# Layers 1 and 2 of a graph network: loops replaced by written-out instructions on four engines

## The chip, the cores and the metric

One core of one Trainium2 chip. The time is the device time of one launch in microseconds (us), the median of several runs. In rows and text PE is TensorE's matmul and PEld its weight load, DVE is VectorE, ACT is ScalarE, POOL is GpSimd and SP is SyncE; a q behind the name is the engine's sequencer.

## The reference

```python
def sage(h, w_self, w_neigh, b):
    agg = segment_sum(h[src], dst, num_segments=n) * inv_deg
    return h @ w_self + agg @ w_neigh + b
h = relu(layernorm(x))                 # 100000 nodes x 128
h = relu(sage(h, ws0, wn0, b0))        # 128 -> 256
h = relu(sage(h, ws1, wn1, b1))        # 256 -> 256
out = x + sage(h, ws2, wn2, b2)        # 256 -> 128
```

The graph has 150000 edges sorted by target: 50000 between random nodes and one from each node to itself. All numbers are float32.

## The kernel before

The kernel is written per engine: each engine has one instruction stream, and semaphores order them. The nodes are cut into 392 pairs of 2 x 128 nodes. Layer 0 goes through the pairs and writes, per node, the two products p (for neighbours) and q (for the node itself) to a table in HBM. Layer 1 does the same with that table and writes z and y. Layer 2 goes through 264 triples of 3 x 128 nodes and writes the output. A preamble (until about 80 us) finds each tile's edges between different nodes; these are few, so that one gather of 128 rows serves a tile in layers 0 and 1, and two gathers serve a triple in layer 2.

In layer 1 a pair passes through these steps, by line:

- VectorE copies the pair's two columns of row numbers into one of four `gather_at` slots (L1146). It first waits until the gathers of the slot's last use have landed.
- GpSimd starts two indirect gathers with them (L646), into one of four `nbr` slots, after TensorE has summed that slot's last rows. SyncE loads the pair's own q rows (L484).
- ScalarE builds a selection matrix (L802, L810) and splits the gathered rows in a high part (L723); VectorE makes the low part (L1156).
- TensorE multiplies with the selection (L1539, L1540, L1543: 4 matmuls), VectorE scales and adds the own rows (L1166), TensorE transposes (L1566: 4), ScalarE and VectorE split the result (L826, L1325), and TensorE does the dense product with W2 (L1445: 12 matmuls of high and low parts).
- ScalarE and VectorE take z and y out of PSUM (L817, L1336) and SyncE stores them (L509).

The engines run these steps of different pairs at once: in one turn TensorE handles pairs n, n-3 and n-1, VectorE n, n-4, n-5, n-7 and n-9. In layer 2 VectorE copies row numbers at L1353, GpSimd gathers at L659, TensorE sums (L1580, L1583), VectorE adds (L1361, L1366, L1378), and ScalarE's queue stores.

All streams are in program order. How a stream is laid out is decided by two helpers: `peeled` writes a step out once for each pair, with constant addresses and constant semaphore counts; `looped` puts four steps (one per slot) in a hardware loop, where the pair number is a register, so that addresses and counts are worked out by register instructions. `pipeline` writes out the first `rounds` times four steps, loops over the rest, and writes out the tail of `lag` steps.

In the kernel before SyncE's stream is written out in all layers. The other four engines use `pipeline` in layers 1 and 2, with `rounds` 2 (GpSimd, TensorE, ScalarE in layer 2), 3 (ScalarE in layer 1, VectorE in layer 2) or 4 (VectorE in layer 1). Layer 0 has loops of its own. Between the layers every store of one layer is waited for before the next begins its gathers, and a branch on a flag skips code for graphs of a more general kind.

Of the kernel before, what the change touches and what calls it, by code (L numbers as in the profile page):

```python
# [20 lines left out]
PAIRS = -(-N_NODES // (PAIR * SLOTS)) * SLOTS  # L21
# [4 lines left out]
TRIPLES = -(-NODE_TILES // (3 * SLOTS)) * SLOTS  # L26
# [50 lines left out]
def peeled(step, first, last, total, slots=SLOTS):  # L77

    for n in range(first, last):
        step(Step(n // slots, n % slots, total, False, slots))  # L80


def looped(eng, step, first_use, last_use, total, slots=SLOTS):

    with eng.Fori(first_use, last_use) as i:
        for slot in range(slots):
            step(Step(i, slot, total, True, slots))


def pipeline(eng, step, total, lag, rounds=2, slots=SLOTS):  # L90

    assert lag < rounds * slots and total % slots == 0
    peeled(step, 0, rounds * slots, total, slots)
    looped(eng, step, rounds, total // slots, total, slots)
    peeled(step, total, total + lag, total, slots)


def build(nc, x, src, dst, dst_starts, windows, ws0, wn0, b0, ws1, wn1, b1, ws2, wn2, b2, out):
# [14 lines left out]
    with ExitStack() as ctx:  # L113
# [274 lines left out]
        def triple_rows(table, s):  # L388

            return table.rearrange("(j r) f -> r j f", j=3)[bass.ds(s.n * P, P), :, :]  # L390
# [136 lines left out]
        def _(pool):  # L527
# [63 lines left out]
            def general(pass_no):  # L591
                with pool.If(pool.value_load(general_flag[0:1, 0:1], min_val=0, max_val=1) != 0):
                    general_sums(pass_no)
# [44 lines left out]
            def gathers(layer, table, rows_in, freed, width):  # L638
                def gather(s):
                    if s.has(SLOTS):  # L640

                        pool.wait_ge(freed, s.back(SLOTS).n + 1)
                    pool.wait_ge(layer.index_copied, s.n + 1)
                    pool.sem_inc(pool_may_go, 1)
                    for j in range(2):
                        pool.indirect_dma_start(rows_in[s.slot][0:SLOT_ROWS, j, 0:width], None, table,  # L646
                                                bass.IndirectOffsetOnAxis(gather_at[s.slot][0:SLOT_ROWS, j:j + 1], axis=0),
                                                bounds_check=last_half_row, oob_is_err=False
                                                ).then_inc(layer.gathered[s.slot], 16)
                pipeline(pool, gather, PAIRS, 0)  # L650

            def triple_gathers(s):
                if s.has(SLOTS):
# [21 lines left out]
            all_stored(pool, L0.stored, SLOT_USES)  # L675
            general(1)
            gathers(L1, p_table, nbr, L1.summed, H)
            all_stored(pool, L1.stored, SLOT_USES)
            general(2)
            pipeline(pool, triple_gathers, TRIPLES, 0)  # L680

        @block.scalar
        def _(act):
# [112 lines left out]
            def layer1(first):  # L796
# [24 lines left out]
                if t.live():  # L821

                    act.wait_ge(L1.turned, t.n + 1)
                    if t.has(2):
                        act.wait_ge(L1.dense_done, t.back(2).n + 1)
                    act.activation(hid_hi[t.half][:, :, :], l1_turn[t.half].rearrange("p (k n) -> p k n", k=2),  # L826
                                   ACT.Relu).then_inc(L1.hi_ready, 1)
            pipeline(act, layer1, PAIRS, 5, rounds=3)


            def layer2(s):
# [14 lines left out]
                if u.live():  # L846
                    act.wait_ge(L2.rows_ready, u.n + 1)
                    act.dma_start(triple_rows(out, u), triple_out[u.slot]).then_inc(L2.stored[u.slot], 16)
            pipeline(act, layer2, TRIPLES, 3)

        @block.vector
        def _(dve):
# [307 lines left out]
            def means(layer, s, width, added):  # L1160

                dve.wait_ge(layer.summed, s.n + 1)
                if s.has(2):
                    dve.wait_ge(layer.turned, s.back(2).n + 1)
                for j in range(2):
                    last = dve.scalar_tensor_tensor(agg[s.half][:, j, 0:width],  # L1166
                                                    row_sums[s.slot][:, j * H:j * H + width],
                                                    inv_degree[:, bass.ds(s.n * 2 + j, 1)],
                                                    added[:, j, 0:width], op0=ALU.mult, op1=ALU.add)
                last.then_inc(layer.agg_ready, 1)  # L1170
# [144 lines left out]
            def layer1(first):  # L1315
# [25 lines left out]
                if s.live():  # L1341
                    dve.wait_ge(L1.own_loaded[s.slot], (s.use + 1) * 16)
                    means(L1, s, H, own[s.slot])
            pipeline(dve, layer1, PAIRS, 9, rounds=4)

            general(2)

# [31 lines left out]
                                      ALU.add).then_inc(L2.rows_ready, 1)  # L1379
            dve.tensor_copy(b2_held, b2_rows[:, :]).then_inc(L2.b2_put, 1)  # L1380
            dve.wait_ge(L2.b2_put, 1)
            pipeline(dve, layer2, TRIPLES, 6, rounds=3)

        @block.tensor
        def _(pe):
# [141 lines left out]
            def layer1(s):  # L1527
# [31 lines left out]
                if t.live():  # L1559
# [6 lines left out]
                            last = nc.tensor.matmul(l1_turn[t.half][:, at:at + P], agg[t.half][:, j, m * P:(m + 1) * P],  # L1566
                                                    ident[:, :], is_transpose=True, start=True, stop=True)
                    last.then_inc(L1.turned, 1)
            pipeline(pe, layer1, PAIRS, 3)

            general(2)

            def layer2(s):
# [10 lines left out]
                                            triple_select[s.half][:, SHARED + j, :],  # L1584
                                            triple_rows_in[s.slot][:, j, :], start=j == 0, stop=j == SHARED - 1)
                last.then_inc(L2.summed, 1)
            pipeline(pe, layer2, TRIPLES, 0)


INPUTS = ["x", "src", "dst", "dst_starts", "windows", "L0_gnn_ws0", "L0_gnn_wn0", "L0_gnn_b0", "L0_gnn_ws1", "L0_gnn_wn1", "L0_gnn_b1",  # L1590
# [36 lines left out]
```

## Time and profile before

| what | value |
|---|---|
| median of 3 runs | 3845.57 us (3840.11 to 3855.55) |
| profiled execution, its own time | 3837.3 us |
| its span in the trace | 3835.5 us |
| instructions recorded | 100978 |
| busy share PE / PEld / DVE / ACT / POOL | 91 / 82 / 87 / 80 / 67% |
| HBM read and written | 451 and 361 MB |
| granted clock of TensorE, mean | 0.923 |

Times in the trace count from the start of the span. An engine is busy while it executes; register, branch and semaphore instructions and the issue of plain transfers are not counted as busy. The granted clock is a share of TensorE's 2.4 GHz. "issue" as what ended an idle time means that the engine waited for nothing that the profile shows.

### The profile page before, as it was taken

Reading aid. Unit: us, or ns where it says so; the run is one execution under the profiler, and the core shown is the slowest. Engines: PE = TensorE matmul, PEld = TensorE weight load, DVE = VectorE, ACT = ScalarE, POOL = GpSimd, SP = SyncE. Lnnn points to the kernel's source line nnn. Section 1 sums busy time; section 2 is a strip of 40 time slices with the busy share of each in tenths; the row PEclk is TensorE's granted clock in tenths of the full one; section 3 lists DMA queues with packets and bytes.
Section 4 is the critical chain, followed back from the end, with each engine's and each line's share of the span. In section 5 each row is a group of like instructions: output and inputs, shape, how many; then the busy total and the mean of one; then the engine's idle time right before and its main releaser. Section 6 shows DMA issues by size and latency. Waiting matters only on the chain. (4 is left out here: it accounts for less than half of the span.)

```text
span 3835.5 us, 100978 instructions
## 1 busy us (share of the span) xinstructions
PE 3503.3 (91%) x22513; PEld 3162.4 (82%) x22513; DVE 3342.0 (87%) x9695; ACT 3085.1 (80%) x8036; POOL 2557.9 (67%) x3691
## 2 busy tenths in 40 slices
PE   1999999999999999999998999999999986777777
PEld 1888888888888888888887999998999976666666
DVE  7999999999999999999986888988988977777777
ACT  4888888888888888888886877878887867777777
POOL 2666666666666666666555777777777767777776
PEclk9999999999999999999999999999999986566555
DMA  2444444444444444444444888888888879999998
GB/s 75 138 143 143 144 142 144 143 144 144 144 143 144 143 142 143 142 143 144 141 145 143 247 245 247 249 248 244 247 246 246 249 216 263 262 262 266 262 265 249
DMA packets 828104, 727.99 MB, mean 190 GB/s; under 512 B 90198, under 2 KB 699614, under 8 KB 827918
## 3 DMA queue, kind: packets, MB, share of 16 engines
q1 hardware_dynamic: 642069, 570.14, 45.9%
q0 software_dynamic: 80336, 104.91, 11.5%
q10 hardware_dynamic: 105600, 51.92, 4.5%
q8 instruction: 26, 0.43, 0.1%
q14 instruction: 73, 0.59, 0.0%
HBM read 451.32 MB, written 361.23 MB: 212 GB/s over the span
## 5 line engine op out<-in xcount | busy, mean ns | idle before, releaser
L1445 PE MATMUL ps_out<-w_hi,hid_hi 128*128 128x512 f32 (+1 forms) x3136 | 1142.3, 364 | 27.3 <-DVE layer_mem L1336 24.7
L610 POOL DMA_INDIRECT loaded_rows<-in_x,gather_at x784 | 904.0, 1153 | 390.2 <-issue 241.7
L1445 PE MATMUL ps_out<-w_hi,hid_lo 128*128 128x512 f32 (+1 forms) x3136 | 1054.6, 336 | 0.0
L1445 PE MATMUL ps_out<-w_lo,hid_hi 128*128 128x512 f32 (+1 forms) x3136 | 1049.7, 335 | 0.0
L646 POOL DMA_INDIRECT layer_mem<-pq_rows,gather_at x784 | 788.2, 1005 | 273.2 <-issue 215.7
L1445 PEld LDWEIGHTS ps_out<-w_hi,hid_hi 128*128 128x128 f32 x3136 | 589.3, 188 | 135.4 <-issue 51.6
L659 POOL DMA_INDIRECT layer_mem<-zy_rows,gather_at x528 | 526.0, 996 | 182.3 <-issue 141.3
L1445 PEld LDWEIGHTS ps_out<-w_hi,hid_lo 128*128 128x128 f32 x3136 | 588.8, 188 | 68.8
L1445 PEld LDWEIGHTS ps_out<-w_lo,hid_hi 128*128 128x128 f32 x3136 | 591.1, 188 | 55.1
L750 ACT ACTIVATE layer_mem<-ps_hid,b_col 128x256 f32<-128x256 f32 x784 | 329.1, 470 | 211.4 <-PE ps_hid L1445 193.7
L837 ACT ACTIVATE layer_mem<-iota_row,triple_node 128x128 f32<-128x128 f32 x1056 | 337.3, 390 | 154.3 <-DVE layer_mem L1378 57.5
L1445 PE MATMUL ps_hid<-cat_hi,w_hi 128*128 128x256 f32 x1568 | 438.5, 280 | 3.6 <-DVE cat_lo L1251 3.4
L1445 PE MATMUL ps_hid<-cat_lo,w_hi 128*128 128x256 f32 x1568 | 435.6, 278 | 0.0
L1445 PE MATMUL ps_hid<-cat_hi,w_lo 128*128 128x256 f32 x1568 | 435.2, 278 | 0.0
L1325 DVE SCALAR_TENSOR_TENSOR hid_lo<-ps_out,hid_hi 128x512 fp32r<-128x512 f32 x392 | 270.6, 690 | 102.9 <-ACT hid_hi L826 90.6
L779 ACT ACTIVATE h_own<-loaded_rows,shift,rstd 128x128 f32<-128x128 f32 x784 | 340.8, 483 | 3.4 <-POOL shift L623 3.3
L1184 DVE BATCH_NORM_STATS2 stats<-loaded_rows 128x6 f32<-128x256 f32 x784 | 300.4, 424 | 48.3 <-DMA loaded_rows<-in_x,gather_at 28.4
L779 ACT ACTIVATE h_nbr<-loaded_rows,shift,rstd 128x128 f32<-128x128 f32 x784 | 340.8, 483 | 0.0
L723 ACT ACTIVATE nbr_hi<-layer_mem 128x256 fp32r<-128x256 f32 x392 | 163.1, 416 | 220.9 <-DMA layer_mem<-pq_rows,gather_at 219.1
L1240 DVE SCALAR_TENSOR_TENSOR layer_mem<-layer_mem,self_scale,ps_out 128x256 f32<-128x256 f32 x784 | 334.4, 467 | 0.9 <-issue 0.7
L1445 PEld LDWEIGHTS ps_hid<-cat_hi,w_hi 128*128 128x128 f32 x1568 | 295.1, 188 | 26.7 <-DVE cat_lo L1251 11.4
L1445 PEld LDWEIGHTS ps_hid<-cat_lo,w_hi 128*128 128x128 f32 x1568 | 295.0, 188 | 17.0
(172 smaller groups left out, 8817.2 us busy)
## 6 DMA issues: line engine op xcount, KB each, us to landing
pq_rows<-layer_mem SPq DMA_DIRECT2D x392, 512.0 KB, 3.2
loaded_rows<-pq_rows SPq DMA_DIRECT2D x392, 256.0 KB
zy_rows<-layer_mem SPq DMA_DIRECT2D x392, 256.0 KB
loaded_rows<-zy_rows SPq DMA_DIRECT2D x264, 192.0 KB, 4.1
layer_mem<-in_x SPq DMA_DIRECT2D x264, 192.0 KB
out_rows<-layer_mem ACTq DMA_DIRECT2D x264, 192.0 KB
loaded_rows<-in_x SPq DMA_DIRECT2D x392, 128.0 KB, 2.2
loaded_rows<-in_x,gather_at POOLq DMA_INDIRECT x784, 2.9
```

Of the source, the lines that this page charges most:

```text
L610: pool.indirect_dma_start(raw[s.slot][0:rows, 2 + j, :], None, table, bass.IndirectOffsetOnAxis(gather_at[s.slot][0:rows, j:j + 1], axis=0 ...
L646: pool.indirect_dma_start(rows_in[s.slot][0:SLOT_ROWS, j, 0:width], None, table, bass.IndirectOffsetOnAxis(gather_at[s.slot][0:SLOT_ROWS, ...
L659: pool.indirect_dma_start(triple_rows_in[s.slot][:, j, :], None, z_table, bass.IndirectOffsetOnAxis(gather_at[s.slot][:, j:j + 1], axis=0) ...
L723: act.activation(nbr_hi[s.half][:, 0:tiles, 0:width], nbr[s.slot][:, 0:tiles, 0:width], ACT.Copy).then_inc(layer.nbr_hi_ready, 1)
L750: last = act.activation(h1[t.half][:, m, :], ps_hid[t.half][:, m * PAIR:(m + 1) * PAIR], ACT.Relu, bias=b0_col[:, m:m + 1])
L779: last = act.activation(rows, raw[t.slot][:, j, :], ACT.Relu, bias=shift[t.half][:, j:j + 1], scale=rstd[t.half][:, j:j + 1])
L837: last = act.activation(triple_distance[s.half][:, b, :], iota_row[:, :], ACT.Abs, scale=-1.0, bias=triple_node[:, bass.ds(s.n * (2 * SHAR ...
L1184: last = dve.bn_stats(stats[t.half][:, k, :], raw[t.slot][:, 2 * k:2 * k + 2, :].rearrange("p j f -> p f j"))
L1240: last = dve.scalar_tensor_tensor(q_out[t.slot][:, j, :], p_out[t.slot][:, j, :], self_scale[:, bass.ds(t.n * 2 + j, 1)], ps_out[t.half][: ...
L1325: dve.scalar_tensor_tensor(hid_lo[t.half][:, :, :], l1_turn[t.half].rearrange("p (k n) -> p k n", k=2), 0.0, hid_hi[t.half][:, :, :].bitca ...
L1445: ins = nc.tensor.matmul(o, a, b, start=n == 0, stop=n == len(terms) - 1)
```

## The change

Eight calls of `pipeline` become calls of `peeled` over all pairs or triples and the tail: GpSimd's, ScalarE's, VectorE's and TensorE's streams of layers 1 and 2 are written out from first to last. Steps, their order on each engine, the semaphores and the buffers stay the same. Layer 0 and SyncE's stream are not touched.

```diff
--- before.py
+++ after.py
@@ -647,7 +647,7 @@
                                                 bass.IndirectOffsetOnAxis(gather_at[s.slot][0:SLOT_ROWS, j:j + 1], axis=0),
                                                 bounds_check=last_half_row, oob_is_err=False
                                                 ).then_inc(layer.gathered[s.slot], 16)
-                pipeline(pool, gather, PAIRS, 0)
+                peeled(gather, 0, PAIRS, PAIRS)
 
             def triple_gathers(s):
                 if s.has(SLOTS):
@@ -677,7 +677,7 @@
             gathers(L1, p_table, nbr, L1.summed, H)
             all_stored(pool, L1.stored, SLOT_USES)
             general(2)
-            pipeline(pool, triple_gathers, TRIPLES, 0)
+            peeled(triple_gathers, 0, TRIPLES, TRIPLES)
 
         @block.scalar
         def _(act):
@@ -825,7 +825,7 @@
                         act.wait_ge(L1.dense_done, t.back(2).n + 1)
                     act.activation(hid_hi[t.half][:, :, :], l1_turn[t.half].rearrange("p (k n) -> p k n", k=2),
                                    ACT.Relu).then_inc(L1.hi_ready, 1)
-            pipeline(act, layer1, PAIRS, 5, rounds=3)
+            peeled(layer1, 0, PAIRS + 5, PAIRS)
 
 
             def layer2(s):
@@ -846,7 +846,7 @@
                 if u.live():
                     act.wait_ge(L2.rows_ready, u.n + 1)
                     act.dma_start(triple_rows(out, u), triple_out[u.slot]).then_inc(L2.stored[u.slot], 16)
-            pipeline(act, layer2, TRIPLES, 3)
+            peeled(layer2, 0, TRIPLES + 3, TRIPLES)
 
         @block.vector
         def _(dve):
@@ -1341,7 +1341,7 @@
                 if s.live():
                     dve.wait_ge(L1.own_loaded[s.slot], (s.use + 1) * 16)
                     means(L1, s, H, own[s.slot])
-            pipeline(dve, layer1, PAIRS, 9, rounds=4)
+            peeled(layer1, 0, PAIRS + 9, PAIRS)
 
             general(2)
 
@@ -1379,7 +1379,7 @@
                                       ALU.add).then_inc(L2.rows_ready, 1)
             dve.tensor_copy(b2_held, b2_rows[:, :]).then_inc(L2.b2_put, 1)
             dve.wait_ge(L2.b2_put, 1)
-            pipeline(dve, layer2, TRIPLES, 6, rounds=3)
+            peeled(layer2, 0, TRIPLES + 6, TRIPLES)
 
         @block.tensor
         def _(pe):
@@ -1566,7 +1566,7 @@
                             last = nc.tensor.matmul(l1_turn[t.half][:, at:at + P], agg[t.half][:, j, m * P:(m + 1) * P],
                                                     ident[:, :], is_transpose=True, start=True, stop=True)
                     last.then_inc(L1.turned, 1)
-            pipeline(pe, layer1, PAIRS, 3)
+            peeled(layer1, 0, PAIRS + 3, PAIRS)
 
             general(2)
 
@@ -1584,7 +1584,7 @@
                                             triple_select[s.half][:, SHARED + j, :],
                                             triple_rows_in[s.slot][:, j, :], start=j == 0, stop=j == SHARED - 1)
                 last.then_inc(L2.summed, 1)
-            pipeline(pe, layer2, TRIPLES, 0)
+            peeled(layer2, 0, TRIPLES, TRIPLES)
 
 
 INPUTS = ["x", "src", "dst", "dst_starts", "windows", "L0_gnn_ws0", "L0_gnn_wn0", "L0_gnn_b0", "L0_gnn_ws1", "L0_gnn_wn1", "L0_gnn_b1",
```

## Rows read from the trace of the kernel before

**Rows 1.** Busy us (xcount) by engine, granted clock, DMA share, GB/s, of the three layers.
```profile
80.00:2040.00 1960.00, 1954.04 (x12392) 1748.90 (x12392) 1814.83 (x5192) 1670.99 (x4267) 1218.74 (x2333) 1.00 0.42 142
2100.00:3100.00 1000.00, 973.05 (x7509) 910.68 (x7508) 893.43 (x2628) 803.14 (x2253) 755.67 (x752) 1.00 0.83 246
3140.00:3820.00 680.00, 491.45 (x2076) 427.30 (x2077) 497.63 (x1552) 513.05 (x1290) 518.66 (x521) 0.59 0.94 262
```

**Rows 2.** Groups of GpSimd, 2266 to 2320 and 3230 to 3280 us.
```profile
L646 POOL DMA_INDIRECT layer_mem<-pq_rows,gather_at x42 | 41.9, 998 | 12.8 <-issue 10.4 <-DVE gather_at L1146 2.4
...
L659 POOL DMA_INDIRECT layer_mem<-zy_rows,gather_at x40 | 39.8, 996 | 12.2 <-issue 9.4 <-DVE gather_at L1353 1.8 <-PE ps_turn L1583 0.6
```

**Rows 3.** Timeline of TensorE's weight loads: start us, us, engine, line.
```profile
2606.19 0.46 PEld L1566 LDWEIGHTS ps_out<-ident,layer_mem 128*128 128x128 f32 x4
...
2608.71 0.46 PEld L1566 LDWEIGHTS ps_out<-ident,layer_mem 128*128 128x128 f32 x4
```

**Rows 4.** Waits, 2100 to 3100 us: us in total, times, longest.
```profile
ACT nbr_hi L723 <- DMA layer_mem<-pq_rows,gather_at: 194.2, 278, 2.5
...
PEld ps_out L1445 <- issue: 48.7, 119, 1.2
...
POOL layer_mem L646 <- DVE gather_at L1146: 38.8, 106, 1.8
```

**Rows 5.** Waits, 3130 to 3800 us.
```profile
DVE gather_at L1353 <- DMA layer_mem<-zy_rows,gather_at: 178.9, 185, 9.2
```

**Rows 6.** Timeline of GpSimd, first and last gathers of a layer.
```profile
2041.18 1.42 POOL L610 DMA_INDIRECT loaded_rows<-in_x,gather_at  x1 [0.30 <-ACT h_nbr L779]
...
2074.96 1.02 POOL L646 DMA_INDIRECT layer_mem<-pq_rows,gather_at  x1 [19.10 <-issue]
...
2081.51 1.00 POOL L646 DMA_INDIRECT layer_mem<-pq_rows,gather_at  x1 [0.30 <-issue]
...
3116.24 1.00 POOL L646 DMA_INDIRECT layer_mem<-pq_rows,gather_at  x1 [0.30 <-issue]
3136.33 0.99 POOL L659 DMA_INDIRECT layer_mem<-zy_rows,gather_at  x1 [19.09 <-issue]
...
3824.55 1.00 POOL L659 DMA_INDIRECT layer_mem<-zy_rows,gather_at  x1 [0.30 <-issue]
```

**Rows 7.** Sequencer records of the loops' own line, 2119 to 3100 us: ns min/median/max.
```profile
L85 POOLq COMPARE_BRANCH  x92: 45/45/45, 2125.0 to 3092.0; - x92
...
L85 PEldq COMPARE_BRANCH  x92: 207/208/208, 2125.2 to 3091.4; - x92
```

**Rows 8.** Timeline of GpSimd, three of the eleven long gaps.
```profile
2226.18 1.00 POOL L646 DMA_INDIRECT layer_mem<-pq_rows,gather_at  x1 [2.10 <-issue]
...
3086.89 1.00 POOL L646 DMA_INDIRECT layer_mem<-pq_rows,gather_at  x1 [1.88 <-issue]
...
3284.38 1.00 POOL L659 DMA_INDIRECT layer_mem<-zy_rows,gather_at  x1 [1.02 <-issue]
```

**Rows 9.** GpSimd's group, 2100 to 3100 us.
```profile
L646 POOL DMA_INDIRECT layer_mem<-pq_rows,gather_at x752 | 755.7, 1005 | 244.5 <-issue 189.0 <-DVE gather_at L1146 38.8 <-PE ps_hid L1543 9.8
```

**Rows 10.** Instruction packets, MB, share: 2119-3100, 2092-2113, 2594-2596 us.
```profile
q14 instruction: 5, 0.04, 0.0%
...
q8 instruction: 2, 0.03, 0.7%
...
q14 instruction: 1, 0.01, 1.2%
```

**Rows 11.** Timeline of TensorE's weight loads in layer 1's written-out start.
```profile
2092.98 0.19 PEld L1445 LDWEIGHTS ps_out<-w_hi,hid_hi 128*128 128x128 f32 x1
2093.09 0.19 PEld L1445 LDWEIGHTS ps_out<-w_lo,hid_hi 128*128 128x128 f32 x1
```

**Rows 12.** Timeline of SyncE's transfers.
```profile
2595.13 0.37 SPq L484 DMA_DIRECT2D loaded_rows<-pq_rows  x1
2595.55 0.46 SPq L509 DMA_DIRECT2D zy_rows<-layer_mem  x1
```

## The prediction

> **What bounds the kernel now.** I first cut the span into its three layers with busy time, granted clock and DMA share [rows 1]. Layer 0 runs until 2040 us with TensorE busy 1954 of 1960 us; none of its code is touched. Layer 1 fills 2100 to 3100 us: TensorE 97%, VectorE 89%, ScalarE 80%, GpSimd 76%, DMA 83%. Layer 2 fills 3140 to 3820 us: no compute engine above 77%, the DMA engines at 94%; TensorE's granted clock is 1.00 (2.4 GHz) in the first two and 0.59, a mix of both levels, in layer 2. By shares alone one would name TensorE for layer 1 and the DMA engines for layer 2.
>
> The groups of GpSimd's gathers say otherwise [rows 2]. In a stretch of layer 1 a gather is busy 998 ns with (12.8 / 42) = 0.305 us before the next one, so one gather each (41.9 + 12.8) / 42 = 1.302 us. In layer 2 it is (39.8 + 12.2) / 40 = 1.300 us. A pair of layer 1, and a triple of layer 2, needs two gathers: 2.604 and 2.600 us.
>
> Then I compared TensorE's own step. When it is not held up, the transposes of one pair start 2.52 us after those of the pair before [rows 3]. So TensorE could do a pair in 2.52 us and the gathers allow one each 2.60 us. The waits of layer 1 agree: ScalarE's first reader of gathered rows (L723) waits 194 us for their DMA, while TensorE's largest entry is 49 us in 119 pieces [rows 4]. In layer 2 the slot copy at L1353 waits 179 us for gathers [rows 5]. TensorE's 97% is thus the trace of an engine that follows 0.08 us per pair behind the real bound.
>
> Last I took the first and last gather of each layer [rows 6]. Layer 1: 2074.96 to 3116.24 us, 1041.3 us for 783 steps; at 1.302 us they would be 1019.5, so 21.8 us are above the floor. Layer 2: 3136.33 to 3824.55 us, 688.2 us for 527 steps, against 686.2 at 1.302 us: 2.0 us above. All that this change can give back inside the two layers, if a gather keeps its price, is 23.8 us.
>
> **The change part by part.**
>
> *GpSimd.* Removed per four pairs: a loop end whose branch is 45 ns [rows 7], and the register work behind addresses and waits. These run on the sequencer while a gather is being made (998 ns), so they are already hidden. What would change the time is the 0.305 us between gathers. Is that loop work? The trace has the written-out form too: the first eight pairs of layer 1 are outside the loop in the kernel before, and the gather of 2081.51 us, one of theirs, has the same 0.30 us before it [rows 6]; two gathers of one pair have no register work between them in the source either. So I book 0 for the floor. Bounds: 0 to 0.01 us per gather, the scatter of such steps (up to 13 us over 1312 gathers); I take 0.
>
> *The long gaps.* Seven times in layer 1 and four times in layer 2 GpSimd pauses between the two gathers of one pair; 2.10 and 1.88 us in layer 1, 1.02 us the first of layer 2 [rows 8]. They stand at the 113th step of each layer and each 108 steps after it; 108 steps are 13.5 rounds of the loop, so the loop does not make them. Less 0.305 us each, the seven of layer 1 (1.51 to 2.10 us) are 11.3 us of the 21.8 above the floor, the four of layer 2 2.3 us. I book 0 for them.
>
> *VectorE, what is left.* The other 10.5 us of layer 1: 752 gathers with a mean of 1005 in place of 998 ns are 5.3 us, and their idle time of 244.5 us less 752 x 0.305 and the 11.3 is 3.8 us [rows 9]; the rest is before 2100 us. The idle time names the slot index that VectorE writes at L1146, 38.8 us in 106 waits, of which 32.3 would pass anyway [rows 4]. VectorE loses its register instructions, and so comes to that copy a little sooner when it was late. I take a third of 10.5, that is -3 us; bounds 0 and -10.5. What of the prolonged gathers goes, I can't tell.
>
> *TensorE and ScalarE.* TensorE's branch at the loop end is 208 ns per four pairs [rows 7], sequencer work while queued matmuls run. Even if all of its waits vanished, it would only wait for gathers instead. Booked at 0: the gathers hide it. If that cover were gone, the loop ends would be worth 98 x 0.208 = 20 us.
>
> *What is added: instructions to load.* In the loops of layer 1, 2119 to 3100 us, the only instruction packets are 5 of 8 KB [rows 10]. SP is already written out and issues 369 + 368 transfers there, 737 to 5 packets: with the rounding some 128 to a packet, 64 bytes an instruction. So they are SP's, and the four looped engines load nothing. After the change they load too. TensorE has 23 matmuls and up to 6 waits a pair: 29 instructions, or 52 if each weight load counts, so 392 x 29 to 52 = 11 to 20 thousand; at 256 to a 16 KB packet 44 to 80 packets. All engines together ran 20.7 thousand instructions in 1000 us of layer 1 and 7.5 thousand in 680 us of layer 2 [rows 1]; with up to half as many again, or in layer 2 as many again, for waits, that is 2 MB and 0.9 MB, against 246 GB/s x 1000 us and 262 GB/s x 680 us: 0.8% and 0.5%, and in layer 2 the DMA engines have 6% left. A load that comes ahead of need costs nothing. That is seen twice. In the written-out start of layer 1 two 16 KB packets came between 2092 and 2113 us, and TensorE's weight loads ran on 0.12 us apart around 2093 us [rows 10, 11]. And SP's 8 KB packet between 2594 and 2596 us left its transfers at 2595.13 and 2595.55 us, one right behind the other [rows 10, 12]. I book +1 us for traffic in layer 2; bounds 0 and +4 (0.5% of 680 us).
>
> *Between layers.* 2041.18 to 2074.96 us and 3116.24 to 3136.33 us, and the end after 3824.55 us, are drained and started by steps that are already outside the loops; 0.
>
> **Sum.** -3 + 1 + 0 = -2 us on the profiled execution, whose own time is 3837.3 us (span 3835.5 and 1.8 around it), so 3835. That execution is 8.3 us under the median of 3845.57; on the median the change is the same: 3843.6 us. A change under 0.5%, 19 us, is about what a measurement of this kernel can't tell from none.
>
> **Weighed against the Trainium skill.** The rows show four engines looping for 980 us without loading anything [rows 10]. "Runtime: NRT & Kernel Launch", section "Instruction fetch mechanics", says that a taken branch to code outside the two held pages stalls for a load, and that kernels prefer full unrolling for it. By that rule the change would be a gain wherever loops reload. The trace disagrees for these loops: their branches load nothing. The same section says that straight code is loaded ahead and mostly hidden, with which the trace agrees.
>
> **The rivals.**
> *Faster: register and loop work does hold the gathers back.* Then the excess above the floor goes as well: -23.8 us, 3822 us (-0.6%). For it: waits on L1146 exist, and VectorE's register work sits before them. Against: 13.6 of the 23.8 us are the periodic gaps, whose places the loop does not explain. Only if these go too does the gain pass 0.5%. Chance 0.10.
>
> *Slower: instruction loads hold TensorE up.* The place is TensorE's queue in layer 1, which has only 2.604 - 2.52 = 0.08 us to spare per pair. One packet of 256 instructions serves 256 / 52 = 4.9 to 256 / 29 = 8.8 pairs, so a stall of more than 0.4 to 0.7 us per packet makes TensorE the bound. The two packets in the start of layer 1 took 0.7% of 16 engines over 21 us, 1.2 us each [rows 10]. Were each fully exposed, layer 1 would grow by (1.2 - 0.7) x 44 = 22 to (1.2 - 0.4) x 80 = 64 us: 3868 to 3910 us, middle 3888. For it: the DMA engines are 83% busy, so a packet can queue. Against: neither of those two packets shows as a pause where TensorE was busy, as around 2093 us [rows 11]. Chance 0.10.
>
> *Slower: GpSimd's own loads.* It has no reserve at all: what stalls it between gathers is added in full. 4 to 5 instructions a pair or triple make (392 + 264) x 4.5 / 128 = 23 packets of 8 KB; at 1.2 us exposed each, +28 us, 3873 us. It passes 0.5% from 0.8 us each. Against: the gather being made (1.0 us) covers most of a load, and loads come ahead on SP. Chance 0.07.
>
> *The loops' removal does nothing at all*, since the compiled waits and gathers cost the same: 3845.6, inside the forecast's range.
>
> **How the numbers follow.** Forecast (within 0.5%, 3826 to 3865) 0.71, gain beyond it 0.11, loss beyond it 0.18 (0.10 and 0.07 and 0.01 for others). The likeliest case has its own range 3832 to 3850. For 8 in 10 the range goes to the fast rival's 3822 and to 3870, where the slower cases begin to be likely.
>
> **What would show it.** Right: gathers of both layers 1.302 us apart, 998 and 996 ns each; the long gaps still 108 steps apart; layer 1's first to last gather 1031 to 1042 us, layer 2's 686 to 690; no entry for loop ends; 60 to 110 more instruction packets in the whole. Wrong: a gap before gathers under 0.29 us (then the gain is larger), TensorE's pair above 2.60 us with waits at a load of instructions, or gathers that start later than 0.31 us after each other at each 128th instruction.

## The result, and the profile after

The kernel with both layers written out took 3857.5 us in the median (3850.7 to 3864.7, 20 runs); the kernel before took 3842.95 us (3836.6 to 3855.6, 20 runs) beside it. The ratio is 1.0037 with a 95% interval of 1.0030 to 1.0043. Forecast were 2 us less; it became 14.6 us more. That is inside the range and inside "within 0.5%", but outside the likeliest case's own range of 3832 to 3850 us, and the sign is wrong by more than the interval. The profiled execution took 3853.33 us with a span of 3851.5, 16.0 us over the span of before.

Where the 16.0 us are is read from the first and last gathers of the layers, in the timeline of GpSimd, changed kernel:

```profile
2074.26 1.02 POOL L646 DMA_INDIRECT layer_mem<-pq_rows,gather_at  x1 [18.96 <-issue]
...
3131.28 1.00 POOL L646 DMA_INDIRECT layer_mem<-pq_rows,gather_at  x1 [0.30 <-issue]
3152.04 1.00 POOL L659 DMA_INDIRECT layer_mem<-zy_rows,gather_at  x1 [19.76 <-issue]
...
3840.39 1.00 POOL L659 DMA_INDIRECT layer_mem<-zy_rows,gather_at  x1 [0.30 <-issue]
```

Against [rows 6], layer 1 went from 1041.3 to 1057.0 us (+15.7), the passage to layer 2 from 20.1 to 20.8, layer 2 from 688.2 to 688.35. All that counts is in layer 1. A second trace of the kernel before (e6 below) has 1044.8 us for layer 1, so the loss there is 12 to 16 us.

The windows' row for 2100 to 3100 us, the group of GpSimd's gathers in that stretch, and the instruction packets of 2119 to 3100 us, changed kernel, answer to [rows 1], [rows 9] and [rows 10]:

```profile
2100.00:3100.00 1000.00, 959.21 (x7399) 899.05 (x7400) 883.13 (x2592) 790.05 (x2222) 749.54 (x742) 1.00 0.83 244
```

```profile
L646 POOL DMA_INDIRECT layer_mem<-pq_rows,gather_at x742 | 750.5, 1011 | 250.8 <-issue 181.6 <-DVE gather_at L1146 55.4 <-PE ps_hid L1543 6.4
```

```profile
q8 instruction: 62, 1.02, 0.5%
q14 instruction: 72, 0.59, 0.2%
```

GpSimd makes 742 gathers in 1000 us where it made 752; ten gathers at 1.302 us are 13.0 us. Clock and DMA share stayed. The undisturbed gap is still 0.30 us; what grew is the mean of a gather (1005 to 1011 ns). The wait for VectorE's index copy grew too (38.8 to 55.4 us), but the second trace of the kernel before has 52.2 us there (its line stands with e6), so this growth shows nothing. And instruction packets are there that were not: 62 of 16 KB on queue 8 and 72 of 8 KB on queue 14, where before had 5 of the latter. The 62 packets of 256 instructions over 981 us, in which 363 pairs of 2.70 us pass, are 44 instructions a pair. The trace has as many on TensorE: 20 matmuls, 20 weight loads and 4 waits a pair. So each weight load counts as one; the prediction's 23 matmuls and 52 instructions were too many.

The waits in the same stretch, changed kernel (us in total, times, longest), against [rows 4]:

```profile
ACT nbr_hi L723 <- DMA layer_mem<-pq_rows,gather_at: 204.7, 244, 3.1
...
PEld ps_out L1445 <- DVE hid_lo L1325: 58.2, 63, 1.4
POOL layer_mem L646 <- DVE gather_at L1146: 55.4, 122, 2.0
...
PEld ps_out L1445 <- issue: 23.9, 78, 0.6
DVE gather_at L1146 <- DMA layer_mem<-pq_rows,gather_at: 12.2, 16, 1.6
```

The engine that loads most, TensorE, shows no pause for its own loads: its idle time without a releaser fell from 48.7 to 23.9 us, and its longest piece from 1.2 to 0.6 us. (Most of the fall is the loop ends that are gone, 92 x 0.208 = 19 us.) What is later is the gathered data: ScalarE waits 10 us longer for it, in fewer waits that are longer in the mean; in four traces whose layer 1 is looped, or written out on GpSimd alone (before, e6, e15, e17), that wait is 193.8 to 194.5 us. TensorE waits longer for VectorE's split (L1325: 24.3 us in the trace of before, 58.2 now).

One such case can be followed. A 16 KB packet (1.7 us of one of the 16 DMA engines) started at 2579.54 us. The timeline after it, changed kernel:

```profile
2585.32 0.42 ACT L723 ACTIVATE nbr_hi<-layer_mem 128x256 fp32r<-128x256 f32 x1 [2.80 <-DMA layer_mem<-pq_rows,gather_at]
2585.32 0.17 DVE L1146 TENSOR_SCALAR gather_at<-slot_index 128x2 int32<-128x2 int32 x1 [1.35 <-DMA layer_mem<-pq_rows,gather_at]
...
2586.35 0.19 PEld L1539 LDWEIGHTS ps_agg<-nbr_hi,select 128*128 128x128 f32 x1 [1.06 <-DVE nbr_lo L1156]
...
2588.14 1.00 POOL L646 DMA_INDIRECT layer_mem<-pq_rows,gather_at  x1 [0.95 <-PE ps_agg L1543]
...
2591.88 1.00 POOL L646 DMA_INDIRECT layer_mem<-pq_rows,gather_at  x1 [1.44 <-DVE gather_at L1146]
```

The gather's rows land late, ScalarE and VectorE stand 2.80 and 1.35 us, TensorE 1.06 us, and 8.6 us after the packet GpSimd waits for a sum and then for an index: (0.95 + 1.44) - 2 x 0.305 = 1.8 us of the pace are lost. One case proves little, so I sorted all steps from gather to gather, without the long gaps, by the time since the last 16 KB packet began: the mean step is 0.02 us over 1.302 within 6 us of it, 0.08 us at 8 to 10 us, 0.06 at 10 to 12, 0.03 to 0.04 after that (about 90 steps in each 2 us). Two later traces with such packets, e7 and e13, also have their largest excess at 8 to 10 us, 0.11 and 0.12.

The landings can be read from the completion records, of which a few per cent are missing. The second gather of a pair lands 3.75 us after its end in the median, 5.93 at most; in before's trace 3.64 and 4.76, in its second trace 3.70 and 4.73. Later than 4.76 us come 13 landings of some 390 in the changed kernel, 14 in e7 and 17 in e13, none in the two traces of before, and 0 to 4 in e14, e15 and e17, where TensorE loads next to nothing in layer 1 either. But e8, which has only packets of 8 KB, has 13 of them too and loses less, so the late landings alone do not set the price.

### The profile page after: what moved, and what is told of

Its sections match the earlier page's. It is cut to its first block and busy times, and to the rows that moved or that the text cites. A ratio compares the mean times of both kernels' runs of the same rounds, so it can differ in the third digit from the quotient of the medians.

```text
span 3851.5 us, 89615 instructions
## 1 busy us (share of the span) xinstructions
PE 3474.6 (90%) x22513; PEld 3142.2 (82%) x22513; DVE 3337.6 (87%) x9695; ACT 3078.8 (80%) x8036; POOL 2565.5 (67%) x3691
## 5 line engine op out<-in xcount | busy, mean ns | idle before, releaser
L1445 PE MATMUL ps_out<-w_hi,hid_hi 128*128 128x512 f32 (+1 forms) x3136 | 1143.8, 365 | 38.9 <-DVE layer_mem L1336 37.8
L1445 PE MATMUL ps_out<-w_hi,hid_lo 128*128 128x512 f32 (+1 forms) x3136 | 1054.5, 336 | 0.0
L1445 PE MATMUL ps_out<-w_lo,hid_hi 128*128 128x512 f32 (+1 forms) x3136 | 1049.7, 335 | 0.0
L1445 PEld LDWEIGHTS ps_out<-w_hi,hid_hi 128*128 128x128 f32 x3136 | 589.3, 188 | 145.2 <-DVE hid_lo L1325 62.2
L1445 PEld LDWEIGHTS ps_out<-w_hi,hid_lo 128*128 128x128 f32 x3136 | 588.9, 188 | 68.7
L1445 PEld LDWEIGHTS ps_out<-w_lo,hid_hi 128*128 128x128 f32 x3136 | 591.1, 188 | 55.4
L1445 PE MATMUL ps_hid<-cat_hi,w_hi 128*128 128x256 f32 x1568 | 438.2, 279 | 3.1 <-DVE cat_lo L1251 3.0
L1445 PE MATMUL ps_hid<-cat_lo,w_hi 128*128 128x256 f32 x1568 | 435.6, 278 | 0.0
L1445 PE MATMUL ps_hid<-cat_hi,w_lo 128*128 128x256 f32 x1568 | 435.2, 278 | 0.0
L1325 DVE SCALAR_TENSOR_TENSOR hid_lo<-ps_out,hid_hi 128x512 fp32r<-128x512 f32 x392 | 269.8, 688 | 101.7 <-ACT hid_hi L826 97.4
L1445 PEld LDWEIGHTS ps_hid<-cat_hi,w_hi 128*128 128x128 f32 x1568 | 295.1, 188 | 25.0 <-DVE cat_lo L1251 9.1
L1445 PEld LDWEIGHTS ps_hid<-cat_lo,w_hi 128*128 128x128 f32 x1568 | 295.0, 188 | 17.2
```

The lines of the kernel that those rows point to most:

```text
L1325: dve.scalar_tensor_tensor(hid_lo[t.half][:, :, :], l1_turn[t.half].rearrange("p (k n) -> p k n", k=2), 0.0, hid_hi[t.half][:, :, :].bitca ...
L1445: ins = nc.tensor.matmul(o, a, b, start=n == 0, stop=n == len(terms) - 1)
```

## The experiments

Two theories. **Theory of the loads:** TensorE's instruction packets get in the way of gather landings, the consumers fall behind, and the gathers wait. **Theory of the spacing** (called theory of the straight line in later expectations): what costs is the register work and the loop turns that are gone, which moved ScalarE's and VectorE's instructions against each other.

The runs fell on chips of two kinds: on one kind the kernel before takes some 3843 us, on the other some 4283 us. A ratio is always against the kernel before on the same chip.

**First set: layer 1 in parts.** Each kernel is the one before with some lines of the change:

```diff
 e1 all four of:
-                pipeline(pool, gather, PAIRS, 0)
+                peeled(gather, 0, PAIRS, PAIRS)
-            pipeline(act, layer1, PAIRS, 5, rounds=3)
+            peeled(layer1, 0, PAIRS + 5, PAIRS)
-            pipeline(dve, layer1, PAIRS, 9, rounds=4)
+            peeled(layer1, 0, PAIRS + 9, PAIRS)
-            pipeline(pe, layer1, PAIRS, 3)
+            peeled(layer1, 0, PAIRS + 3, PAIRS)
 e2 the last pair alone; e3 the first three pairs
```

e4 keeps all loops and adds 78 transfers, one in five pairs, each of 16372 bytes as TensorE's packets have 16384; nobody reads what they bring:

```diff
+    code_like = x.rearrange("n f -> (n f)").rearrange("(a n) -> a n", a=1)[:, 0:4093]
...
                 load_own(L1, q_dram, H, s, L1.agg_ready)
+                if s.live() and s.n % 5 == 4:
+                    sp.wait_ge(code_loaded, 16 * (s.n // 5))
+                    sp.dma_start(code_sink, code_like).then_inc(code_loaded, 16)
```

> Layer 1 alone written out on all four engines, layer 2 looped. Both theories put the loss in layer 1, where the first to last gather went from 1041.3 to 1057.0 us: +15 us against the kernel before (+12 to +18), and the layer 2 part unchanged. If the loss needed layer 2's code as well, under +8 us.

> Layer 1 written out on TensorE only. Theory of the loads (instruction packets, above all TensorE's 16 KB ones, delay the landing of gathers): TensorE has about 1.0 of the 1.6 MB of code loaded in layer 1, so +8 to +14 us. Theory of the spacing (without register work VectorE and ScalarE reach their instructions at other moments and meet GpSimd's gathers more often): TensorE's registers do not touch that, so -3 to +3 us.

> Layer 1 written out on GpSimd, ScalarE and VectorE, TensorE looped. Theory of the loads: only 8 KB packets, 0.6 MB, +2 to +6 us. Theory of the spacing: nearly the whole loss, +11 to +17 us.

> The loops of before stay; SyncE adds, for every fifth pair of layer 1, one transfer of 16372 bytes in one piece into one partition that nothing reads (78 in all), at the rate of TensorE's code packets. Theory of the loads: one long packet on one DMA engine at a time is enough to delay gathers, +6 to +15 us. Theory of the spacing: nothing changes on the engines, 0 to +3 us.

Measured, on a chip where before takes 4283.67 us: e1 4251.29 (0.9928, 0.9914 to 0.9941), e2 4282.43 (0.9993, 0.9984 to 1.0002), e3 4260.06 (0.9947, 0.9933 to 0.9961), e4 4285.53 (1.0004, 0.9995 to 1.0014). Nothing was slower and two were clearly faster, e1 by 32 us where 12 to 18 us more were expected: this chip could not show the loss at all. So the full change was run again.

> The whole change again, beside the kernel before. On the chip of the four runs before this one the kernel before took 4284 us in place of 3843, and layer 1 written out was faster there. If this run's kernel before is near 3843 us, +11 to +18 us as at first; if it is near 4284 us, -25 to -40 us, layer 1's -31 and little from layer 2.

On another chip of that kind it took 4214.68 us against 4279.82: 0.9837 (0.9819 to 0.9855). The sign of the change is not the same on all chips. (No chip of the experiments was measured at two times, so whether this belongs to the chip or to the moment is not shown.) What differs is seen in the kernel with layer 2 alone written out (e12 below), whose layer 1 is that of before; its windows' row, and its groups of ScalarE, 2100 to 3100 us:

```profile
2100.00:3100.00 1000.00, 785.91 (x5876) 723.64 (x5877) 692.17 (x2059) 635.20 (x1767) 588.45 (x590) 0.99 0.68 193
```

```profile
L826 ACT ACTIVATE hid_hi<-ps_out 128x512 fp32r<-128x512 f32 x295 | 174.8, 593 | 206.5 <-PE ps_out L1566 194.6 <-remote 11.5 <-issue 0.3
...
L723 ACT ACTIVATE nbr_hi<-layer_mem 128x256 fp32r<-128x256 f32 x294 | 119.9, 408 | 8.1 <-DMA layer_mem<-pq_rows,gather_at 5.7 <-issue 1.4 <-remote 0.8
```

Nearly the same granted clock (0.99 against 1.00) and the same operations (L826 593 ns, 589 in before's trace), but 590 gathers in 1000 us in place of 752, and ScalarE hardly waits for gathered rows (5.7 us against 194.2 in [rows 4]). It waits for TensorE's transposes, VectorE waits 295 us for ScalarE (L1325 for L826), TensorE's matmuls 78 us for VectorE (L1445 for L1325), and GpSimd 267 us for TensorE's sums. So the pace there is not set by the gathers but by a chain through the engines; which link makes it longer than on the other chips is not shown. That the loops' register work lies on this chain is argued from the gains: they come with ScalarE's, VectorE's and GpSimd's part (e3), TensorE's alone brings none (e2), and late gathers can hide there. The gain of layer 1 (0.72%, e1) and that of layer 2 (0.83%, e12 below) add up to 1.55%, against 1.63% for the whole.

**Second set: the same kernels on a chip of 3840 us.** e6 is the kernel before once more, e7 is e2, e8 is e3, e9 is e4.

> The kernel before itself, one profile. On a chip like that of the first comparison (3843 us): layer 1's gathers 1041 us from first to last, 1.30 us apart. On a chip like those of the last five runs (4280 us): layer 1 near 1325 us and layer 2 near 838 us, and z's copy to SBUF (L817) waiting for the store of four pairs before.

> TensorE alone written out in layer 1, again, for a chip on which the kernel before takes 3843 us. Theory of the loads (instruction packets delay the landing of gathers, which set the pace there): +8 to +14 us, as TensorE has 1.0 of the 1.6 MB of code. Theory of the spacing (without register work VectorE and ScalarE reach their instructions at other moments): -3 to +3 us. On a chip of 4280 us: -3 to +3 us as before.

> GpSimd, ScalarE and VectorE written out in layer 1, TensorE looped, again, for such a chip. Theory of the loads: 0.6 MB in 8 KB packets, +2 to +6 us. Theory of the spacing: +11 to +17 us. On a chip of 4280 us: -20 to -26 us as before.

> The loops of before with 78 idle transfers of 16372 bytes in one piece from SyncE's queue in layer 1, again, for such a chip. Theory of the loads: +6 to +15 us. Theory of the spacing: 0 to +3 us.

e6 took 3837.54 us (3845.48 beside it); its layer 1, first to last gather, took 1044.8 us where the other trace of before had 1041.3, so one trace resolves a layer to some 4 us. Its group of gathers shows how far the entry for L1146 goes by itself:

```profile
L646 POOL DMA_INDIRECT layer_mem<-pq_rows,gather_at x750 | 753.4, 1005 | 247.6 <-issue 184.6 <-DVE gather_at L1146 52.2 <-PE ps_hid L1543 4.9
```

Of the others, e7 took 3854.32 against 3839.83, 1.0039 (1.0025 to 1.0052). e8: 3842.70, 1.0015 (1.0006 to 1.0024). e9: 3848.11, 1.0021 (1.0012 to 1.0031). TensorE alone gives a loss as large as that of the whole change; with e8's it would be 0.54%, so the parts do not simply add. The profiled execution of e7 was the slowest of its six (3864.91 us) and that of e9 the fastest of its ten (3841.11 us), so their traces show the way more than the size. The group of GpSimd's gathers and the instruction packets, e7:

```profile
L646 POOL DMA_INDIRECT layer_mem<-pq_rows,gather_at x736 | 747.4, 1015 | 253.4 <-issue 176.1 <-DVE gather_at L1146 53.2 <-PE ps_hid L1543 9.7
```

```profile
q8 instruction: 62, 1.02, 0.5%
q14 instruction: 5, 0.04, 0.0%
```

The theory of the loads expects TensorE's part to be nearly all and does get it (14.5 us where 8 to 14 were expected); idle transfers with every loop in place cost 0.21%, about half. The theory of the spacing, which allowed e9 at most 3 us, can't explain its 8. But e7 adds packets and removes register work together, and e9 is an imitation: its 78 transfers took 0.68 us of a DMA engine each in the mean, the 66 packets of the changed kernel's TensorE in layer 1 1.26 us. What is missing is TensorE's packets with its loop in place.

**Third set: a loop too long to hold.** TensorE's layer 1 stays a loop with counts in registers; a round holds 16 pairs (e10, e14), 8 (e11) or 96 (e13, some 4300 instructions by its trace):

```diff
-            pipeline(pe, layer1, PAIRS, 3)
+            def wide(uses):
+                peeled(layer1, 0, 2 * SLOTS, PAIRS)
+                with pe.Fori(0, (PAIRS // SLOTS - 2) // uses) as i:
+                    for m in range(uses * SLOTS):
+                        layer1(Step(i * uses + (2 + m // SLOTS), m % SLOTS, PAIRS, True, SLOTS))
+                peeled(layer1, PAIRS, PAIRS + 3, PAIRS)
+            wide(4)      # e11: 2, e13: 24
```

> Only TensorE's layer 1 differs: it stays a loop with counts in registers, but a round holds sixteen pairs (some 830 instructions) where it held four (some 208). Theory of the loads (TensorE's instruction packets hold gather landings up): the loop is longer than what TensorE can keep, so the packets come back with the loop still in place. About as many q8 instruction packets as with TensorE written out alone (91), layer 1 some 15 to 22 us longer, and the time 10 to 17 us over that of before on a chip where before takes some 3843 us. Theory of the straight line (what costs is the absence of register work and of loop turns): most of the register work is still there, so the time stays within 4 us of before, packets or none. On a chip where before takes some 4280 us, both theories expect within 4 us, as with TensorE written out alone there.

> As the run with sixteen pairs per round, with eight (some 416 instructions). The theory of the loads leaves open whether such a round still stays where TensorE keeps it, and so makes its forecast of the pair of numbers: if the q8 instruction packets stay near the 26 of before, the time is that of before within 4 us; if they are near 91, it is 10 to 17 us over it. The theory of the straight line expects before's time within 4 us at either count of packets.

Both fell on a chip of 4283 us: 4280.73 (0.9993, 0.9983 to 1.0002) and 4281.10 (0.9996, 0.9987 to 1.0005), with 28 and 27 packets on queue 8 in the whole, where I had expected e10 to load. My guess of what TensorE holds was too small, and my count of its instructions too large: the traces have some 730 from one return to the next where 830 were expected (e10 and e14), and such a loop is held. So e13 was made six times as long, and e10 became its control.

> TensorE's layer 1 is a loop again with counts in registers, now with 96 pairs (some 5000 instructions) per round and four rounds. A round of sixteen pairs brought no further instruction packets (28 on q8, 26 in before), this one is six times as long. Theory of the loads: the packets come back (some 85 to 91 on q8) with the loop and the register arithmetic in place, and on a chip where before takes some 3843 us the time is 10 to 17 us over before. Theory of the straight line: within 4 us of before there, whatever the packets. Where before takes some 4280 us both expect within 4 us.

> The loop of sixteen pairs per round again, which had 28 q8 packets. It has a quarter of the turns of before's loop and no packets. Theory of the loads: within 4 us of before on any chip. Were it the loop's turns that keep the spacing, the time would rise on a chip where before takes some 3843 us, by up to the 15 us of TensorE written out.

Both ran on one chip of 3844.12 us. e14, loop and no packets: 3848.85, 1.0009 (1.0000 to 1.0018). e13, loop and packets: 3874.76, 1.0082 (1.0069 to 1.0096). Their groups and packets, e14 and then e13:

```profile
L646 POOL DMA_INDIRECT layer_mem<-pq_rows,gather_at x746 | 752.2, 1008 | 247.7 <-issue 176.2 <-DVE gather_at L1146 58.4 <-PE ps_hid L1543 8.5
```

```profile
q8 instruction: 2, 0.03, 0.0%
q14 instruction: 5, 0.04, 0.0%
```

```profile
L646 POOL DMA_INDIRECT layer_mem<-pq_rows,gather_at x723 | 735.5, 1017 | 265.1 <-issue 172.9 <-DVE gather_at L1146 52.8 <-PE ps_agg L1543 19.1
```

```profile
q8 instruction: 69, 1.13, 0.5%
q14 instruction: 5, 0.04, 0.0%
```

The theory of the straight line expected e13 at before's time, and falls. But e13 is 31 us slower, twice what was expected. The timeline at one of the three returns of its loop shows the rest, e13:

```profile
2633.72 1.00 POOL L646 DMA_INDIRECT layer_mem<-pq_rows,gather_at  x1 [0.31 <-issue]
2638.04 0.19 PEld L1539 LDWEIGHTS ps_agg<-nbr_hi,select 128*128 128x128 f32 x1 [4.17 <-issue]
2639.08 0.42 ACT L723 ACTIVATE nbr_hi<-layer_mem 128x256 fp32r<-128x256 f32 x1 [3.76 <-PE ps_agg L1543]
2639.87 1.00 POOL L646 DMA_INDIRECT layer_mem<-pq_rows,gather_at  x1 [5.15 <-PE ps_agg L1543]
```

TensorE stands 4.17 us with no releaser, and GpSimd then waits 5.15 us for its sum. The three returns (TensorE 3.20, 4.17 and 4.21 us) gave gaps of 3.10, 5.15, 1.78, 4.84 and 2.23 us before gathers, 15.6 us without the 0.305 of each. The other 15 us are as many as e7's 14.5, now with the loop in place. Measured against its control e14 in place of before, e13 is 25.9 us slower, and 10 us are left beside the returns; by layer 1 in the two traces (1081.3 against 1049.2 us) it is 16. So the packets cost 10 to 16 us with the loop in place.

The Trainium skill, "Runtime: NRT & Kernel Launch", section "Instruction fetch mechanics", gives TensorE room for 2048 instructions, and says that a taken branch to code outside the current window of two pages stalls for a fetch. The traces agree with the room and with the stall: a loop of 730 instructions loaded nothing, and one of 4300 stood 3.2 to 4.2 us at each return. They disagree with two pages of 256 instructions as the limit for TensorE, since 730 were held. The loops of before, which the prediction took for a disagreement, speak neither way: TensorE's has some 190 instructions by its trace, fewer than one page.

**Fourth set: what is left of the change.** e12 and e15 write out layer 2 alone; e16 is the whole change without TensorE's layer 1; e17 is GpSimd's layer 1 alone:

```diff
 e12, e15:
-            pipeline(pool, triple_gathers, TRIPLES, 0)
+            peeled(triple_gathers, 0, TRIPLES, TRIPLES)
 and the lines of layer2 on act, dve and pe, as in the change
 e16, against the changed kernel:
-            peeled(layer1, 0, PAIRS + 3, PAIRS)
+            pipeline(pe, layer1, PAIRS, 3)
```

> Layer 2 alone written out, on GpSimd, TensorE, ScalarE and VectorE; layer 1 keeps its loops. On a chip where before takes some 3843 us: both theories expect within 4 us of before, since layer 2 of the changed kernel took 688.3 us from first to last gather against 688.2. On a chip where before takes some 4280 us: 25 to 38 us less than before, all of it in layer 2, whose gathers there ran from first to last in 803.8 us with everything written out and 836 to 840 us with layer 2 looped.

> Layer 2 alone written out on all four engines, again. Where before takes some 4280 us it took 35 us less. Where before takes some 3843 us: the theory of the loads expects at most +4 us, as layer 2 has only 17 more q8 packets and 36 more q14 packets in some 690 us and the changed kernel's layer 2 took 688.3 us against 688.2; a gain over 4 us is expected by neither theory.

> The whole change except TensorE's layer 1, which keeps its loop. Where before takes some 3843 us: the theory of the loads expects the +6 us that layer 1's other three engines cost (3842.7 against before in that run, ratio 1.0015) and nothing for layer 2, so 3843 to 3851; that is below the changed kernel's 3857.5. Where before takes some 4280 us: the gain of layer 1's other three engines (23 us) and that of layer 2 (35 us) add to some 58 us, 4222, against the 4215 of the full change. The theory of the straight line expects the same on the second kind of chip, and on the first most of the full change's 15 us, since the register work of three engines is gone.

> Only GpSimd's layer 1 is written out. Its gathers' gaps without a wait were 0.305 us in a loop and written out alike, and its packets lie ahead of use. Both theories expect within 4 us of before where before takes some 3843 us; where it takes some 4280 us, where ScalarE's and VectorE's chain sets the pace, within 4 us too.

e12, chip of 4283 us: 4247.82, 0.9917 (0.9903 to 0.9931), with layer 2's gathers from first to last in 806.2 us (838.6 in e10, where it is looped). The other three on chips of 3842 to 3844 us: e15 3840.70, 0.9998 (0.9989 to 1.0006); e16 3847.34, 1.0014 (1.0005 to 1.0023); e17 3842.12, 1.0001 (0.9992 to 1.0010). The groups of GpSimd's gathers, 2100 to 3100 us, of e16 and of e17:

```profile
L646 POOL DMA_INDIRECT layer_mem<-pq_rows,gather_at x748 | 753.2, 1007 | 247.8 <-issue 182.3 <-DVE gather_at L1146 51.1 <-PE ps_hid L1543 9.3
```

```profile
L646 POOL DMA_INDIRECT layer_mem<-pq_rows,gather_at x753 | 758.3, 1007 | 243.1 <-issue 184.1 <-DVE gather_at L1146 45.0 <-PE ps_hid L1543 5.5
```

Leaving TensorE's layer 1 in its loop takes the loss from 0.37 to 0.14%, measured on two chips of one kind. GpSimd's part is free. Layer 2's part is free on one kind of chip and worth 0.83% on the other: of the versions tried it is the one that loses on neither and gains on one. None was clearly faster than the kernel before on a chip of 3843 us, and none than the full change on one of 4283 us.

## Why the prediction was wrong, step by step

- **The bound: right.** Layer 1 goes at the pace of gathers, and those came 0.30 us apart after 1.00 us in all versions wherever nothing waited. (On the chips of 4283 us it does not hold, see e12.)
- **GpSimd at 0: right,** shown by e17. Its packets for layer 1 were 8 or 9 of 8 KB (81 on queue 14 against 73 and 72 in the two traces of before). The rival's count of 23 for both layers is 14 for this one. They cost nothing that the run resolves.
- **The long gaps at 0: right.** Layer 1's stand at the same steps, 108 apart, and sum to 11.7 us where they were 11.3.
- **VectorE at -3: not borne out.** The term was a third of 10.5 us in one trace; layer 1 of the same kernel differs by 3.5 us from one trace to the other, and its wait on L1146 is 38.8 us in one and 52.2 in the other. In e8, where GpSimd, ScalarE and VectorE are written out without TensorE, it is 60.0 us, so it did not shrink. e8 costs 0.15% (0.06 to 0.24) and e17 nothing, so ScalarE's and VectorE's parts together cost some 3 to 6 us (e8 by the medians and by the ratio). Whether by their packets of 8 KB or by their changed spacing was not tried.
- **TensorE at 0, and the loads at +1 in layer 2 only: the step that failed.** "A load that comes ahead of need costs nothing" was read from pauses of the engine that loads. That half holds: TensorE did not pause. But the load is a transfer like others, and I asked only what it does to its own engine and to the total traffic (0.5 to 0.8%), not what it does to a gather in flight. In a stream of gathers with no reserve, the term is about +14.5 us (e7), or 10 to 16 us (the part of e13 that is not its returns). I looked for the effect in layer 2, where the DMA engines are fullest; it is nil there (688.35 against 688.2 us; e15).
- **The rival of TensorE's loads** had the sign and the place, not the way: it priced a pause of TensorE's queue at 22 to 64 us. That pause exists only when code is not loaded ahead, at e13's returns.
- **Packets.** 44 to 80 were worked out for TensorE in layer 1, from 23 matmuls a pair; the traces have 20 and in all 44 instructions, which gives 392 x 44 / 256 = 67, and e7 has 65 more than before (91 against 26). For all engines 60 to 110 were forecast and 188 came (108 + 179 against 26 + 73): ScalarE's, VectorE's and layer 2's were undercounted.
- **Between the layers at 0: right** to 0.7 us.

Why so little delays so much is argued from these numbers, not shown by a run: TensorE needs 2.52 us for a pair that comes each 2.604, so it makes up 0.08 us a pair, and a lateness of 1 us takes 12 pairs, 31 us, to go. The packets come each 16 us. How much of TensorE's cost is the traffic as such stays open: e9 imitated the size of the packets, but its transfers held a DMA engine only half as long each (53 us in all against 83), and its trace has a single landing later than 4.76 us.

## What to carry to other kernels

Writing a loop out replaces register work by instruction traffic. On the chips of 3843 us the packets of one engine cost more than all of this kernel's loop ends and register work gave back. Ask of such a change not only whether the engine that loads is late, but whose data is in flight then: if the pace is set by transfers that arrive just in time, keep the engine with the most instructions in a loop that is short enough to be held. Where the pace was set by a chain through the engines' queues, the same edit was a gain (e1, e5, e12); so know which of the two bounds the kernel on the chip that it will run on, and try the parts one by one.

## What was not expected of the hardware

- The same kernel takes 3843 us on some chips and 4283 us on others, at nearly the same granted clock (1.00 and 0.99 in layer 1) and the same duration of its operations; a pair of layer 1 takes 2.66 us on the one and 3.39 on the other (1325 us for its 391 steps), and the full change is 0.37% slower on the one and 1.63% faster on the other. Why the chain through the engines is longer there wasn't settled: of the 12544 completion records of layer 1's gathers 3315 are there in e12's trace, 12126 in before's.
- TensorE's stream has 44 instructions for a pair's 20 matmuls, and comes in packets of 16 KB; the other engines' come in 8 KB. It held a loop of some 730 instructions without a load, and returning to the start of one of some 4300 stopped it for 3.2 to 4.2 us.
- With TensorE's stream written out (0.5% of the DMA engines' time in packets) the kernel took 14.5 us longer, over 1% of layer 1 (e7).
